# Expert stage of an attention and mixture-of-experts kernel: ten row buffers, an earlier norm and an earlier register load

## The chip, the cores and the metric

The kernel runs on one NeuronCore of a Trainium2 chip. A time is what the device takes for one execution, in microseconds (us); the time of a kernel is the median of several executions.

## The reference

4096 tokens of 128 values pass through a cross attention and then through a layer of 8 experts of which each token uses one. What matters here is the second part:

```python
idx = jnp.argmax(router_probs, axis=-1)            # one expert of 8 for each token
xn = (xt - mu) * jax.lax.rsqrt(var + LN_EPS) * ln_g + ln_b
h = jax.nn.relu(jnp.einsum('te,td,edf->tf', onehot, xn, W1) + b1[idx])     # 128 -> 512
y = jnp.einsum('te,tf,efd->td', onehot, h, W2) + b2[idx]                   # 512 -> 128
x = x + y * gates
```

## The kernel before

The first two thirds of the program compute attention and router, and scatter each token's row (its values, gate, number and the two numbers of its norm) into a table in DRAM, `rows_dram`, in which the rows of one expert stand together. A small table, `slot`, is then worked out on VectorE (DVE): for each of 39 slots (`SLOTS`) of 128 rows, which expert it belongs to and where in `rows_dram` it begins. All 8 experts' weights lie in SBUF (`WA`).

The expert stage runs over the 39 slots. Nothing but the order of code on each engine and the semaphores between them sets the order. For slot s:

- SyncE (SP) reads the slot's first row number into a register and loads 128 rows into `G[s % R]`, with R = 6 buffers. Buffer s % R is free once the result of slot s − R has been written to `out` (the waits on `g_in` and `o_out` ahead of line 287).
- DVE makes the normalised rows: `norm(s)`, line 685, from `G` into `xh`, which has two buffers.
- TensorE (PE) transposes them (line 827, "tr" below), ScalarE (ACT) copies the transpose into `xg` (line 468).
- PE multiplies with W1 in 8 matmuls (line 834, "up"); ACT applies bias and relu to half of the result (line 477), DVE to the other half in two instructions (line 697).
- PE multiplies with W2 in 8 matmuls (line 845, "down").
- DVE adds the bias (`yb`, line 704), applies the gate and the residual (`ot`, line 706; R buffers too), and GpSimd (POOL) scatters `ot` to `out` (line 388).
- The weights of the slot's expert are first copied from `WA` into one of three buffers `WR`: W1 by ACT (line 461), W2 and the biases by DVE (`stage_w2`, line 677). For the address, DVE first reads the expert's number from `slot` into a register (`value_load`, line 674).

PE's order in a step is tr(s+1), up(s), down(s−1). DVE's order in a step is:

```python
dve.wait_ge(b_up, s + 1)
norm(s + 2)
wait(dve, b_dn, s - 1)
...                                  # two relus of slot s, L697
dve.wait_ge(b_dn, t + 1)             # t = s - 1
...                                  # yb L704, ot L706 of slot s - 1
stage_w2(s + 2)                      # value_load L674, then the copy L677
```

Of the kernel before, what the change touches and what calls it, by code (L numbers as in the profile page):

```python
# [12 lines left out]
NB, S, D, H = 64, 64, 128, 16  # L13
DK = D // H
E, F = 8, 512
T = NB * S
P = 128
NP = T // P
FC = F // P
SLOTS = (T + E * (P - 1)) // P  # L20
# [14 lines left out]
def wait(eng, sem, value):  # L35

    if value > 0:
        eng.wait_ge(sem, value)
# [31 lines left out]
def build(nc, x, xT, ctxT, mask, wa, wb, wc, wpk, out):  # L70
# [4 lines left out]
    with ExitStack() as ctx:  # L75
        def sb(name, shape, dt=F32):
            return ctx.enter_context(nc.sbuf_tensor(name, shape, dt))

        def sem(name):
            return ctx.enter_context(nc.semaphore(name))  # L80
# [12 lines left out]
        ident = sb("ident", [P, P])  # L93
# [67 lines left out]
        slot = sb("slot", [1, 2, SLOTS], I32)  # L161


        R, NW, LA, NA = 6, 3, 2, 2
        xh = sb("xh", [P, 2, P])
        WA = sb("WA", [P, E, WP])
        WR = sb("WR", [P, NW, WP])
        G = sb("G", [P, R, RW])
# [5 lines left out]
        ps = ctx.enter_context(nc.psum_tensor("ps", [P, 8, 512], F32))  # L174
# [33 lines left out]
        b_tx, b_xg, b_up = sem("b_transposed"), sem("b_xT"), sem("b_up")  # L208
# [11 lines left out]
        def w1_of(s, c):  # L220
            return WR[:, s % NW, P * c:P * c + P]

        def w2_of(s, c):
            return WR[:, s % NW, F + D * c:F + D * c + D]

        def b1_of(s, c):
            return WR[:, s % NW, F + FC * D + c:F + FC * D + c + 1]

        def b2_of(s):
            return WR[:, s % NW, F + FC * D + FC:WP]  # L230

        def h_ps(s, c):
            b, k = (0, c) if c < NA else (1, c - NA)
            return ps[:, 2 * (s % 2) + b, P * k:P * k + P]
# [246 lines left out]
        def _(dve):  # L481
            v = nc.vector
# [187 lines left out]

            dve.wait_ge(s_we, 128)

            def stage_w2(s):
                ex = dve.value_load(slot[0:1, 0, s:s + 1], min_val=0, max_val=E - 1)  # L674
                wait(dve, b_dn, s - NW + 1)
                wait(dve, b_ra, NA * (s - NW + 1))
                v.tensor_copy(WR[:, s % NW:s % NW + 1, F:WP], WA[:, bass.ds(ex, 1), F:WP]).then_inc(b_w2, 1)  # L677

            stage_w2(0)
            stage_w2(1)  # L680
            def norm(t):
                q = t % R
                dve.wait_ge(g_in[q], 16 * (t // R + 1))
                wait(dve, b_tx, t - 1)
                v.tensor_scalar(xh[:, t % 2, :], G[:, q, 0:D], G[:, q, D + 3:D + 4], G[:, q, D:D + 1],  # L685
                                ALU.mult, ALU.add).then_inc(b_xh, 1)

            norm(0)
            norm(1)
            for s in range(SLOTS + 1):  # L690
                if s < SLOTS:
                    dve.wait_ge(b_up, s + 1)
                    if s + 2 < SLOTS:
                        norm(s + 2)
                    wait(dve, b_dn, s - 1)
                    for c in range(NA, FC):
                        v.tensor_scalar(hT[:, s % 2, P * c:P * c + P], h_ps(s, c), b1_of(s, c), 0.0,  # L697
                                        ALU.add, ALU.max).then_inc(b_rd, 1)
                if s >= 1:
                    t = s - 1  # L700
                    q = t % R
                    wait(dve, o_out[q], 16 * (t // R))
                    dve.wait_ge(b_dn, t + 1)
                    v.tensor_tensor(out=yb[:, t % 2, :], in0=ps[:, 6 + t % 2, 0:D], in1=b2_of(t), op=ALU.add).then_inc(b_y, 1)  # L704
                    dve.wait_ge(b_y, t + 1)
                    v.scalar_tensor_tensor(out=ot[:, q, :], in0=yb[:, t % 2, :], scalar=G[:, q, D + 2:D + 3],  # L706
                                           in1=G[:, q, 0:D], op0=ALU.mult, op1=ALU.add).then_inc(b_o, 1)
                if s + 2 < SLOTS:
                    stage_w2(s + 2)

        @block.tensor
        def _(pe):
            mm = nc.tensor.matmul

            for i in range(FIRST, LAST):
                if 0 <= i < NP:
                    q, c = i // GP % 2, P * (i % GP)
# [104 lines left out]
            for s in range(-1, SLOTS + 1):  # L822
                if s + 1 < SLOTS:
                    t = s + 1
                    pe.wait_ge(b_xh, t + 1)
                    wait(pe, b_xg, t - 1)
                    nc.tensor.transpose(ps[:, 4 + t % 2, 0:P], xh[:, t % 2, :], ident[:]).then_inc(b_tx, 1)  # L827
                if 0 <= s < SLOTS:
                    pe.wait_ge(b_w1, s + 1)
                    pe.wait_ge(b_xg, s + 1)  # L830
                    wait(pe, b_ra, NA * (s - 1))
                    wait(pe, b_rd, (FC - NA) * (s - 1))
                    for c in range(FC):
                        last = mm(h_ps(s, c), w1_of(s, c), xg[:, s % 2, :], start=True, stop=True)  # L834
                    last.then_inc(b_up, 1)
                if s >= 1:
                    t = s - 1
                    wait(pe, b_y, t - 1)
                    pe.wait_ge(b_w2, t + 1)
                    for c in range(FC):  # L840
                        if c < NA:
                            pe.wait_ge(b_ra, NA * t + c + 1)
                        else:
                            pe.wait_ge(b_rd, (FC - NA) * t + c - NA + 1)
                        last = mm(ps[:, 6 + t % 2, 0:D], hT[:, t % 2, P * c:P * c + P], w2_of(t, c),  # L845
                                  start=(c == 0), stop=(c == FC - 1))
                    last.then_inc(b_dn, 1)
# [37 lines left out]
```

## Time and profile before

| | |
|---|---|
| median of 3 runs | 316.54 us (315.61 to 317.49) |
| profiled execution, its own time | 319.22 us |
| its span, first to last instruction | 317.5 us |
| DVE busy | 220.6 us (70%) |
| PE busy | 249.2 us (79%) |
| first `xh` to last scatter's start | 213.42 to 310.38 us |

The profiled execution took 1.7 us more than its span, and 2.7 us more than the median of the others. "Busy" is the time in which an engine had an instruction at work; names such as DVEq stand for an engine's instruction queue, which handles waits and registers.

### The profile page before, as it was taken

How to read it: one execution, taken by the hardware profiler on the slowest of the kernel's cores; microseconds unless marked ns; L12 is line 12 of the kernel's file. 1: busy time of each engine (PE TensorE's matmuls, PEld its weight loads, DVE VectorE, ACT ScalarE, POOL GpSimd, SP SyncE). 2: the span in 40 equal slices, each digit the busy share in tenths (PEclk: the TensorE clock that was granted, in tenths of full speed). 3: DMA queues.
4: the chain of work that ended last, by engine and by line, in shares of the span. 5: the costliest groups of instructions: out<-in, count | busy, mean ns of one | idle time of the engine just before them, and what ended most of it. 6: DMA issues, size and time to landing. Idle time of an engine off the chain costs nothing.

```text
span 317.5 us, 8922 instructions
## 1 busy us (share of the span) xinstructions
PE 249.2 (79%) x3112; PEld 200.7 (63%) x3112; DVE 220.6 (70%) x674; ACT 177.3 (56%) x342; POOL 141.2 (44%) x158
## 2 busy tenths in 40 slices
PE   1488988998979989789898665008899999899880
PEld 0336665765857767658576664007788888788870
DVE  6517864785886979958798735814877877877870
ACT  1527784777584767576655310007667667667640
POOL 3812250541456476464672617720444434444441
PEclk9999997997997999999999955556999999999996
DMA  7999999999999940000000101111122121121110
GB/s 228 298 245 223 273 232 238 253 265 261 263 294 267 255 109 22 10 23 15 11 28 2 37 0 37 43 40 39 43 49 59 54 68 42 51 67 53 48 29 0
DMA packets 49611, 36.31 MB, mean 114 GB/s; under 512 B 3087, under 2 KB 45460, under 8 KB 49568
## 3 DMA queue, kind: packets, MB, share of 16 engines
q1 hardware_dynamic: 46864, 31.11, 43.3%
q0 software_dynamic: 2272, 4.27, 4.2%
q8 instruction: 25, 0.41, 0.5%
q10 hardware_dynamic: 432, 0.38, 0.5%
q14 instruction: 18, 0.15, 0.2%
HBM read 14.11 MB, written 22.09 MB: 114 GB/s over the span
## 4 chain that ended last, share of the span: by engine, by line
PE 38%; DVE 31%; issue 14%; ACT 5%; DVEq 3%; DMA 3%; POOL 2%; POOLq 1%; SPq 1%; ACTq 0%
PE ps L742 8%; PE ps L753 7%; DVE Pr L569 5%; PE ps L729 4%; DVE mx L549 4%; DVE xh L685 4%; DVE hT L697 4%; PE ps L803 3%; DVE ot L706 3%; PE ps L760 2%; PE ps L766 2%; PE ps L725 2%; PE ps L780 2%; DVE yb L704 2%; DVEq L674 2%
## 5 line engine op out<-in xcount | busy, mean ns | idle before, releaser
L388 POOL DMA_INDIRECT out<-ot,G x39 | 39.8, 1021 | 62.6 <-DVE ot L706 61.6
L415 ACT ACTIVATE PT<-ps 128x512 f32<-128x512 f32 x64 | 35.2, 595 | 49.7 <-PE ps L753 49.6
L549 DVE TENSOR_REDUCE mx<-ps 128x16 f32<-128x1024 f32 x32 | 39.2, 1224 | 28.6 <-PE ps L729 28.1
L742 PEld LDWEIGHTS ps<-VB,PT 128*64 128x64 f32 x1024 | 34.1, 140 | 27.1 <-issue 27.1
L742 PE MATMUL ps<-VB,PT 128*64 128x18 f32 x1024 | 36.9, 214 | 14.7 <-ACT OT L408 7.3
L834 PE MATMUL ps<-xg,WR 128*128 128x128 f32 x312 | 45.1, 289 | 0.0
L845 PE MATMUL ps<-WR,hT 128*128 128x128 f32 x312 | 41.0, 275 | 0.0
L365 POOL TENSOR_TENSOR Kb<-KT,hmask 128x512 f32<-128x512 f32 x32 | 33.2, 1042 | 17.0 <-PE ps L729 16.7
L419 ACT ACTIVATE Pr<-Pr,rowany 128x1024 f32<-128x1024 f32 x32 | 36.7, 1148 | 7.1 <-DVE Pr L569 6.0
L834 PEld LDWEIGHTS ps<-xg,WR 128*128 128x128 f32 x312 | 39.2, 197 | 1.4
L341 POOL DMA_INDIRECT rows_dram<-row,posi x32 | 32.5, 1016 | 14.3 <-DVE row L582 6.5
L569 DVE TENSOR_TENSOR Pr<-ps,mx 128x1024 f32<-128x1024 f32 x32 | 38.8, 1213 | 0.1
L845 PEld LDWEIGHTS ps<-WR,hT 128*128 128x128 f32 x312 | 37.9, 192 | 0.0
L753 PE MATMUL ps<-ident,Pr 128*128 128x128 f32 x256 | 37.5, 293 | 0.1
L468 ACT ACTIVATE xg<-ps,Wa 128x128 f32<-128x128 f32 x39 | 17.9, 458 | 27.4 <-PE ps L827 27.4
L677 DVE COPY WR<-WA 128x644 f32 x39 | 19.4, 496 | 19.8 <-issue 19.8
L461 ACT ACTIVATE WR<-WA 128x512 f32 x39 | 24.6, 630 | 14.9 <-DVE slot L668 7.7
L348 POOL TENSOR_TENSOR row<-ve,half 128x8 f32<-128x8 f32 x8 | 13.3, 1665 | 41.5 <-DVE ve L640 41.5
L753 PEld LDWEIGHTS ps<-ident,Pr 128*128 128x128 f32 x256 | 29.3, 147 | 1.5 <-ACT Pr L419 0.5
L827 PE MATMUL ps<-ident,xh 128*128 128x128 f32 x39 | 13.2, 337 | 20.2 <-DVE xh L685 17.4
L477 ACT ACTIVATE hT<-ps,WR 128x128 f32<-128x128 f32 x78 | 23.8, 355 | 2.2 <-PE ps L834 2.2
L697 DVE TENSOR_SCALAR hT<-ps,WR 128x128 f32<-128x128 f32 x78 | 23.5, 343 | 0.0
(121 smaller groups left out, 379.7 us busy)
## 6 DMA issues: line engine op xcount, KB each, us to landing
rows_dram<-empty SPq DMA_DIRECT2D x32, 528.0 KB, 10.5
WA<-in_wpk SPq DMA_DIRECT2D x8, 578.0 KB
G<-rows_dram SPq DMA_DIRECT2D x39, 66.0 KB, 1.9
X<-in_x SPq DMA_DIRECT2D x8, 256.0 KB, 7.2
C<-in_ctxT SPq DMA_DIRECT2D x8, 256.0 KB, 6.6
XT<-in_xT SPq DMA_DIRECT2D x8, 256.0 KB, 6.5
out<-ot,G POOLq DMA_INDIRECT x39, 2.3
rows_dram<-row,posi POOLq DMA_INDIRECT x32
```

The source lines that it names most:

```text
L341: g.indirect_dma_start(out=rows, out_offset=bass.IndirectOffsetOnAxis(ap=posi[:, r, k:k + 1], axis=0), in_=row[:, r, k, E:E + RW], in_offs ...
L365: g.tensor_tensor(out=Kb[:, p % 3, :, :], in0=KT[:, p // GP % 2, c:c + P][:, None, :].to_broadcast([P, 4, P]), in1=hmask[:, :, None].to_br ...
L388: g.indirect_dma_start(out=out, out_offset=bass.IndirectOffsetOnAxis(ap=G[:, q, D + 1:D + 2].bitcast(I32), axis=0), in_=ot[:, q, :], in_of ...
L415: a.activation(PT[:, p % 2, 512 * m:512 * m + 512], ps[:, 4 + m, :], ACT.Copy).then_inc(freed[4 + m], 1)
L419: a.activation(Pr[:, i % 2, :], Pr[:, i % 2, :], ACT.Exp, scale=rowany[:, 0:1]).then_inc(s_p, 1)
L549: v.tensor_reduce(out=mx[:, i % 2, :], in_=psS.rearrange("p g (i k) -> p g i k", k=S), axis=AX.X, op=ALU.max).then_inc(s_mx, 1)
L569: v.tensor_tensor(out=Pr[:, i % 2, :].rearrange("p (g i k) -> p g i k", g=4, k=S), in0=psS.rearrange("p g (i k) -> p g i k", k=S), in1=mx[ ...
L697: v.tensor_scalar(hT[:, s % 2, P * c:P * c + P], h_ps(s, c), b1_of(s, c), 0.0, ALU.add, ALU.max).then_inc(b_rd, 1)
L742: last = mm(psPV[64 * b:64 * b + 64, 18 * j:18 * j + 18], PT[:, p % 2, 128 * j + 64 * b:128 * j + 64 * b + 64], VB[:, p // GP % 3, 2 * (p ...
L753: last = nc.tensor.transpose(ps[:, 4 + m, 128 * j:128 * j + 128], Pr[:, p % 2, 128 * (4 * m + j):128 * (4 * m + j) + 128], ident[:])
L834: last = mm(h_ps(s, c), w1_of(s, c), xg[:, s % 2, :], start=True, stop=True)
L845: last = mm(ps[:, 6 + t % 2, 0:D], hT[:, t % 2, P * c:P * c + P], w2_of(t, c), start=(c == 0), stop=(c == FC - 1))
```

## The change

Three things are edited. R goes from 6 to 10, so that both `G` and `ot` have ten buffers. `xh` gets a third buffer, and DVE's norm runs three slots ahead of the relus instead of two, behind them instead of ahead of them. The register load of the expert's number is taken out of `stage_w2` and put between relu and norm. The lines below it move by two to five numbers: norm is L687 in the new kernel, relu L698, yb L709, ot L711, the W2 copy L679; the load stays L674.

```diff
-        R, NW, LA, NA = 6, 3, 2, 2
-        xh = sb("xh", [P, 2, P])
+        R, NW, LA, NA = 10, 3, 2, 2
+        xh = sb("xh", [P, 3, P])
...
-            def stage_w2(s):
-                ex = dve.value_load(slot[0:1, 0, s:s + 1], min_val=0, max_val=E - 1)
+            def expert_of(s):
+                return dve.value_load(slot[0:1, 0, s:s + 1], min_val=0, max_val=E - 1)
+
+            def stage_w2(s, ex):
...
-                wait(dve, b_tx, t - 1)
-                v.tensor_scalar(xh[:, t % 2, :], G[:, q, 0:D], G[:, q, D + 3:D + 4], G[:, q, D:D + 1],
+                wait(dve, b_tx, t - 2)
+                v.tensor_scalar(xh[:, t % 3, :], G[:, q, 0:D], G[:, q, D + 3:D + 4], G[:, q, D:D + 1],
...
+            norm(2)
             for s in range(SLOTS + 1):
                 if s < SLOTS:
                     dve.wait_ge(b_up, s + 1)
-                    if s + 2 < SLOTS:
-                        norm(s + 2)
                     wait(dve, b_dn, s - 1)
                     for c in range(NA, FC):
                         v.tensor_scalar(hT[:, s % 2, P * c:P * c + P], h_ps(s, c), b1_of(s, c), 0.0,
                                         ALU.add, ALU.max).then_inc(b_rd, 1)
+                    if s + 2 < SLOTS:
+                        ex = expert_of(s + 2)
+                    if s + 3 < SLOTS:
+                        norm(s + 3)
...
-                    stage_w2(s + 2)
+                    stage_w2(s + 2, ex)
...
-                    nc.tensor.transpose(ps[:, 4 + t % 2, 0:P], xh[:, t % 2, :], ident[:]).then_inc(b_tx, 1)
+                    nc.tensor.transpose(ps[:, 4 + t % 2, 0:P], xh[:, t % 3, :], ident[:]).then_inc(b_tx, 1)
```

On DVE, one step in the middle of the expert stage stood like this before (`b_up`, `b_down` and `b_transposed` count PE's finished ups, downs and transposes, `rows_in4` the landed rows of slot 4; "ISA" are register instructions):

```order
L685 TENSOR_SCALAR xh<-G 128x128 [waits b_transposed,rows_in4,b_up]
L697 TENSOR_SCALAR hT<-ps,WR 128x128 [waits b_down]
L697 TENSOR_SCALAR hT<-ps,WR 128x128
L704 TENSOR_TENSOR yb<-ps,WR 128x128 [waits b_down]
L706 SCALAR_TENSOR_TENSOR ot<-yb,G 128x128 [waits b_y]
L674 TENSOR_LOAD slot
L674 ISA x2
L677 ISA [waits b_relu_act,b_down]
L677 COPY WR<-WA 128x644
```

The same step on DVE in the changed kernel:

```order
L698 TENSOR_SCALAR hT<-ps,WR 128x128 [waits b_down,b_up]
L698 TENSOR_SCALAR hT<-ps,WR 128x128
L674 TENSOR_LOAD slot
L674 ISA x2
L687 TENSOR_SCALAR xh<-G 128x128 [waits b_transposed,rows_in5]
L709 TENSOR_TENSOR yb<-ps,WR 128x128 [waits b_down]
L711 SCALAR_TENSOR_TENSOR ot<-yb,G 128x128 [waits b_y]
L679 ISA [waits b_relu_act,b_down]
L679 COPY WR<-WA 128x644
```

The register load and its two register instructions have moved from between ot and the W2 copy to between relu and norm; norm has moved behind the relus and handles the rows of one slot later. Of the register work only one instruction (L679 ISA) is left between ot and the copy.

At the start of the stage DVE now reads as follows, from the norm of slot 0 to the relus of slot 1:

```order
L687 TENSOR_SCALAR xh<-G 128x128 [waits rows_in0]
L687 TENSOR_SCALAR xh<-G 128x128 [waits rows_in1]
L687 TENSOR_SCALAR xh<-G 128x128 [waits rows_in2]
L698 TENSOR_SCALAR hT<-ps,WR 128x128 [waits b_up]
L698 TENSOR_SCALAR hT<-ps,WR 128x128
L674 TENSOR_LOAD slot
L674 ISA x2
L687 TENSOR_SCALAR xh<-G 128x128 [waits b_transposed,rows_in3]
L679 ISA
L679 COPY WR<-WA 128x644
L698 TENSOR_SCALAR hT<-ps,WR 128x128 [waits b_up]
```

The third norm stood behind the wait for the first up before; it now waits for its rows alone.

## Rows read from the trace of the kernel before

**Rows 1.** The page: TensorE's granted clock in 40 slices, tenths of full speed.

```profile
PEclk9999997997997999999999955556999999999996
```

**Rows 2.** Busy time in a stretch: PE, PEld, DVE, ACT, POOL, then clock, DMA.

```profile
224.00:304.00 80.00, 75.11 (x577) 67.67 (x576) 61.50 (x203) 54.18 (x137) 34.88 (x34) 1.00 0.19 53
```

**Rows 3.** Groups of 224 to 304 us: busy, mean ns, idle before, releaser.

```profile
L677 DVE COPY WR<-WA 128x644 f32 x34 | 16.9, 497 | 17.2 <-issue 17.2
L827 PE MATMUL ps<-ident,xh 128*128 128x128 f32 x34 | 11.2, 328 | 4.9 <-DVE xh L685 2.1
```

**Rows 4.** DVE in order of time: start, us, line, [idle before <- releaser].

```profile
228.32 0.35 DVE L706 SCALAR_TENSOR_TENSOR ot<-yb,G 128x128 f32<-128x128 f32 x1
229.15 0.50 DVE L677 COPY WR<-WA 128x644 f32 x1 [0.48 <-issue]
229.56 0.34 DVE L685 TENSOR_SCALAR xh<-G 128x128 f32<-128x128 f32 x1
229.82 0.60 DVE L697 TENSOR_SCALAR hT<-ps,WR 128x128 f32<-128x128 f32 x2
230.34 0.28 DVE L704 TENSOR_TENSOR yb<-ps,WR 128x128 f32<-128x128 f32 x1
230.65 0.35 DVE L706 SCALAR_TENSOR_TENSOR ot<-yb,G 128x128 f32<-128x128 f32 x1
...
269.63 0.49 DVE L677 COPY WR<-WA 128x644 f32 x1 [0.83 <-issue]
```

**Rows 5.** L674 from 228.3 to 229.1 us: ns min/median/max, first and last start.

```profile
L674 DVEq TENSOR_LOAD <-slot x1: 305/305/305, 228.3 to 228.3; - x1
L674 DVEq FUSED_REGOPS  x1: 190/190/190, 228.7 to 228.7; - x1
```

**Rows 6.** DVE in order of time at slot 0.

```profile
217.47 0.34 DVE L685 TENSOR_SCALAR xh<-G 128x128 f32<-128x128 f32 x1 [2.28 <-PE ps L834]
217.73 0.60 DVE L697 TENSOR_SCALAR hT<-ps,WR 128x128 f32<-128x128 f32 x2
218.25 0.48 DVE L677 COPY WR<-WA 128x644 f32 x1
```

**Rows 7.** L674 from 217.4 to 218.2 us.

```profile
L674 DVEq TENSOR_LOAD <-slot x1: 304/304/304, 217.5 to 217.5; - x1
```

**Rows 8.** PE in order of time, slots 0 to 1.

```profile
215.51 1.92 PE L834 MATMUL ps<-xg,WR 128*128 128x128 f32 x8
217.87 0.47 PE L827 MATMUL ps<-ident,xh 128*128 128x128 f32 x1 [0.44 <-DVE xh L685]
...
219.53 1.06 PE L845 MATMUL ps<-WR,hT 128*128 128x128 f32 x8
220.43 0.27 PE L827 MATMUL ps<-ident,xh 128*128 128x128 f32 x1
220.54 1.06 PE L834 MATMUL ps<-xg,WR 128*128 128x128 f32 x8
221.43 0.83 PE L845 MATMUL ps<-WR,hT 128*128 128x128 f32 x6
```

**Rows 9.** The chain that ended last, 252 to 262 us: start, us, what.

```profile
254.09 0.36 DVE ot L706
...
255.24 2.85 DMA out<-ot,G
...
258.30 1.84 DMA G<-rows_dram
...
260.23 0.13 DVE xh L685
```

**Rows 10.** The end of the program in order of time.

```profile
308.85 0.35 DVE L706 SCALAR_TENSOR_TENSOR ot<-yb,G 128x128 f32<-128x128 f32 x1
309.10 0.97 POOL L388 DMA_INDIRECT out<-ot,G  x1 [0.71 <-issue]
310.38 0.97 POOL L388 DMA_INDIRECT out<-ot,G  x1 [0.30 <-issue]
```

**Rows 11.** Busy time as in Rows 2, a stretch of the attention stage.

```profile
48.00:52.50 4.50, 3.81 (x16) 2.85 (x15) 2.29 (x7) 2.17 (x4) 0.00 (x0) 0.62 1.20 256
```

More of the change, by code:

```diff
@@ L677, in stage_w2 @@
                 v.tensor_copy(WR[:, s % NW:s % NW + 1, F:WP], WA[:, bass.ds(ex, 1), F:WP]).then_inc(b_w2, 1)
-            stage_w2(0)
-            stage_w2(1)
+            stage_w2(0, expert_of(0))
+            stage_w2(1, expert_of(1))
             def norm(t):
```

## The prediction

> **What bounds the kernel now.** I read the busy times by stretch first. From 224 to 304 us the clock of TensorE is granted in full, and in 80 us PE is busy 75.1, DVE 61.5, ACT 54.2, POOL 34.9 us, with the DMA engines at 0.19 [rows 2]. PE looks like the bound, but matmuls are pipelined and their ends are modelled, so I went to the order of time for the length of one slot. From ot to ot it is 228.32 to 230.65, 2.33 us [rows 4]. In that slot DVE has one hole: 0.48 us ahead of the W2 copy, put down to "issue". The grouped view says that the hole is there in every slot: 17.2 us over 34 copies, 0.51 each [rows 3]. Elsewhere DVE starts one instruction right behind the other: ot to copy 0.83, copy to norm 0.41, norm to relu 0.26, two relus 0.52, yb to ot 0.31, which adds up to 2.33 us. So DVE, with its hole, sets the period, and PE waits for it: PE is idle 4.9 us over 34 transposes [rows 3], and the rest of its slack is hidden in the modelled ends.
>
> What the hole is: the register load begins at 228.3, together with ot, takes 0.305, and the register instructions behind it 0.190 and some gaps, so that the copy can start only 0.83 after ot did, although ot needs but 0.35 [rows 4, 5]. The load runs in the instruction queue, beside ot; what shows is the part that ot doesn't cover.
>
> What PE could do without waits is seen where it had none. From the down at 219.53 through tr at 220.43 and up at 220.54 to the next down at 221.43 no idle time stands ahead of any matmul [rows 8]. That is a full slot of 17 matmuls in 1.90 us, 0.112 each.
>
> **The change part by part.**
>
> *The register load.* Behind the relus it has work to hide under. The trace of before has this very order once, at slot 0, where no yb and ot exist: norm at 217.47, relus at 217.73, and the copy at 218.25 right behind them, with no idle time [rows 6]. The load began at 217.5, with the norm, while both relus were still to run [rows 7]. So the queue runs ahead of at least two instructions that wait for their engine. From the start of the load to the first instruction that needs its end are some 0.70 us (the 0.83 of ot to copy less about 0.13 for the one register instruction that stays at the copy). In the new order that instruction is norm, because the queue is in order: norm can start 0.70 after the load, the relus cover 0.52 of this, and a hole of at most 0.18 stays ahead of norm. The load no longer stands ahead of the copy, so ot to copy falls from 0.83 to about 0.27, what relu to copy took at slot 0 (218.25 less the second relu's start, which is 217.73 + 0.26) [rows 6].
>
> *DVE's slot after.* Without any hole: norm 0.26, relus 0.52, yb 0.31, ot 0.27, copy 0.41 = 1.77 us. With the whole hole of 0.18 it is 1.95. PE's slot is 1.90. But the hole shrinks when DVE is late: the wait for up is then already met when the copy starts, the relus and the load are passed on while the copy runs, and the load ends earlier against norm, as at slot 0. So DVE settles at PE's 1.90 and PE becomes the bound. I also looked at what PE would wait for: relu of slot s ends 0.6 to 0.7 after up(s), and down(s) begins about 1.0 after up(s) ended plus another up of 0.9, so over a microsecond is spare there; xh is made a whole slot before tr. yb waits for down(s−1), which ends 0.89 after up(s), and DVE gets there at 0.96 (0.70 + norm 0.26): no new wait. ACT is busy 54.18 of 80 us, 1.58 a slot of 2.33 [rows 2], below 1.90, and none of it moves.
>
> *Norm a slot further ahead, three buffers.* It costs nothing in the steady part: one norm per slot as before, and its new wait is for tr(s+1) (b_transposed at s+2), which stands ahead of up(s) on PE and so has passed when DVE comes out of its wait for up(s). What is queued behind norm is yb, ot and the copy; they would be held if G[s+3] were late (below). At the start it takes one wait away: tr(2) stood idle for 0.44 us for a norm that DVE began only after up(0) [rows 8]; now that norm is done before. These 0.44 us are at the low clock (8 matmuls of up(0) took 1.92, some 0.21 each [rows 8]), two matmuls' worth, which are then done in 0.11 each at the high clock. Gain about 0.2 us: the first down starts at 219.3 instead of 219.53.
>
> *Ten buffers.* The chain from ot(t) over the scatter, its landing and the load of G to norm(t+R) was 254.09 to 260.23, 6.14 us [rows 9], in a slot where it was just late: with R = 6 and norm two ahead there are 3 slots of 2.33 less 1.08 (norm stands that much ahead of ot in its step), 5.9 us. With three ahead and R = 10 there are 6 slots of 1.90 less about 0.6, 10.8 us. It is hidden with 4.6 us to spare. Were R still 6, there would be only 3.2 us for 6.14 and the gain would be lost, so this edit carries the other two. The two or three somewhat longer slots of before (this chain) go too. POOL needs 1.27 us from scatter to scatter when it has nothing to wait for, 309.10 to 310.38 [rows 10], well below 1.90. SP issues the same 39 loads; four more of them go out early, behind those for slots 0 to 5, where nothing is queued behind them but later loads.
>
> *What may not be covered.* Three slots of before were 0.35 longer because DVE's queue stopped for 0.35 at the copy, as at 269.63 with 0.83 idle instead of 0.48 [rows 4]. DVE at 1.77 catches up on a PE at 1.90 with 0.13 a slot, and the spare microsecond between relu and down should hide them. I allow 0.5 us in all for such things.
>
> **The sum.** Before, the last ot started at 308.85 [rows 10]. After: first down at 219.3; 37 slots of 1.90 less 0.11 for the missing last transpose bring the last but one down to 289.5; the last starts 0.89 later, at 290.4, ends 1.06 later, and yb and ot follow at 291.5 and 291.85. The gain is 17.0 us; from ot to the end nothing changes (1.53 us to the last scatter [rows 10], and its landing). The profiled execution's own 319.22 would become 302.2. It was 2.7 above the median, so against the runs it is 316.54 − 17.0 + 0.5 = **300.0 us**.
>
> The Trainium skill has a rule against this placement: "DMA: Bandwidth & Descriptors", section "Latency and other measured facts", gives a register load a floor of about 600 ns. The trace disagrees: 305 ns [rows 5]. By the rule load to norm would be about 1.0 instead of 0.70, DVE's slot 2.25, and by an estimate from that page the time some 312 us.
>
> **The rivals.**
>
> *DVE stays the bound by a little* (0.15). If the relus and the load are passed on only when the copy is done, the hole of 0.18 stays whole: 1.95 us a slot, 37 × 0.05 = 1.9 us more, and the three stops of 0.35 then count too, 1.0 more: 302.4, and up to 304 if gaps of 0.05 come on top. For it speaks that 1.95 and 1.90 are so close; against it, that the load began ahead of the relus at slot 0.
>
> *The change doesn't do what it says: the load waits until the second relu is at work* (0.07), as it began together with ot at 228.3 (where a wait for yb held it, though). Then 0.70 − 0.26 = 0.44 shows ahead of norm, DVE's slot is 1.77 + 0.44 = 2.21, and the gain 37 × 0.12 and the slots of before that waited for rows, some 6 us: 311. The one row at slot 0 speaks against it.
>
> *A transfer chain or POOL becomes the bound* (0.04): with scatters every 1.90 us landing would have to take over 4.6 us longer than the 2.85 of rows 9 to be felt. At half a microsecond a slot it would be 310 or so. The DMA engines at 0.19 speak against it.
>
> *Slower* (0.03): TensorE's clock. A slot of 17 matmuls at the lower clock, 1.2 GHz, is about 3.6 us (0.21 each), 1.7 more than forecast. The clock would have to be low for more than ten slots for the 17 us to be used up. For it speaks that it fell for a while in the attention stage with PE busy 3.81 of 4.50 us [rows 11]; against, that the whole expert stage after 219 us ran at full clock [rows 1], and PE only gets busier.
>
> *No change* within 0.5% (0.02): all of the gain is given back by a wait that I don't see.
>
> **How the numbers follow.** The forecast, PE as the bound, has 0.69, and spans 298.0 (no allowance, and PE's idle time at the start shrinking further) to 302. The range reaches over the first rival, to 305, which holds 0.8. What a measurement of this kernel can tell from no change is about 0.5%, 1.6 us; faster by more has 0.69 + 0.15 + 0.07 + 0.04 = 0.95, the same 0.02, slower 0.03.
>
> **What would show it.** In the new profile: ot to ot 1.90 us in most slots; no idle time ahead of the W2 copy; at most 0.2 ahead of norm; PE without idle time ahead of tr, and tr, up and down following at 0.11 and 0.89; no wait of norm for rows; tr(2) with no wait and the first down near 219.3; last ot near 292. Wrong would be a hole of 0.4 or more ahead of norm, yb waiting for down with DVE then late for the relus so that PE waits for hT, ACT's relu or xg turning up as what PE waits for, or a low clock after 219 us.

## The result, and the profile after

The changed kernel takes 301.52 us (median of 4 executions, 297.93 to 303.73) against 316.85 us of the kernel before beside it (315.61 to 317.49). The ratio is 0.948, with a 95% interval of 0.939 to 0.958. Run a second time, beside two of the experiments and the kernel before at 317.92 us, it was 300.03 us and 0.947 (0.941 to 0.952). All ratios and intervals in this document come from the executions in the faster of two states that the chip shows, and the medians from all executions, so that a ratio is not the quotient of the medians beside it.

The profiles put the gain in the expert stage. From the start of the first norm to the start of the last ot it took 213.42 to 308.85 us before, 95.4 us, and takes 215.11 to 293.36 us now, 78.2 us: 17.2 us less. The profiled execution reached the first norm 1.7 us later than the one of before, in code that is the same in both; how long that first part takes varies from one execution to the next by several us (first norm at 210.8 and at 216.9 us in two profiles of one and the same kernel below). The medians differ by 15.3 us in the first set and by 17.9 in the second, around the 17.2 of the stage. So below I compare this length of the stage, and the total only with its interval.

Busy time by stretch for the changed kernel, to be held against [rows 2] (PE, PEld, DVE, ACT, POOL, granted clock, share of DMA):

```profile
224.00:290.00 66.00, 66.00 (x594) 66.00 (x594) 62.37 (x209) 55.57 (x139) 33.48 (x36) 1.00 0.23 63
```

PE is at work in 66.00 of 66 us. Before, it was 75.1 of 80. The groups of the same stretch, against [rows 3]:

```profile
L679 DVE COPY WR<-WA 128x644 f32 x35 | 17.1, 489 | 0.0
...
L832 PE MATMUL ps<-ident,xh 128*128 128x128 f32 x34 | 9.3, 273 | 0.0
```

The copy has lost its 17.2 us of idle time, and the transpose its 4.9 us. DVE in order of time, against [rows 4]:

```profile
226.25 0.35 DVE L711 SCALAR_TENSOR_TENSOR ot<-yb,G 128x128 f32<-128x128 f32 x1
226.52 0.49 DVE L679 COPY WR<-WA 128x644 f32 x1
226.92 0.61 DVE L698 TENSOR_SCALAR hT<-ps,WR 128x128 f32<-128x128 f32 x2
227.67 0.35 DVE L687 TENSOR_SCALAR xh<-G 128x128 f32<-128x128 f32 x1
227.93 0.28 DVE L709 TENSOR_TENSOR yb<-ps,WR 128x128 f32<-128x128 f32 x1
228.25 0.35 DVE L711 SCALAR_TENSOR_TENSOR ot<-yb,G 128x128 f32<-128x128 f32 x1
...
230.81 0.60 DVE L698 TENSOR_SCALAR hT<-ps,WR 128x128 f32<-128x128 f32 x2
231.34 0.35 DVE L687 TENSOR_SCALAR xh<-G 128x128 f32<-128x128 f32 x1
231.60 0.28 DVE L709 TENSOR_TENSOR yb<-ps,WR 128x128 f32<-128x128 f32 x1
231.92 0.35 DVE L711 SCALAR_TENSOR_TENSOR ot<-yb,G 128x128 f32<-128x128 f32 x1
```

From ot to copy are 0.27 us instead of 0.83. The slot from 226.25 to 228.25 has a hole between relus and norm (relu pair at 226.92, norm at 227.67: 0.75, where 0.52 are needed), the one that ends at 231.92 has none (230.81 to 231.34: 0.53). The queue's rows of the two slots show what differs:

```profile
L674 DVEq TENSOR_LOAD <-slot x1: 428/428/428, 226.8 to 226.8; - x1
...
L674 DVEq TENSOR_LOAD <-slot x1: 310/310/310, 230.6 to 230.6; - x1
```

The register load took 428 ns in the first and 310 in the second, and in both it began while the copy was still at work, 0.1 and 0.2 us ahead of the relus. Over the stage it took 299 to 487 ns (median 311), where it had taken 299 to 420 (median 304) before; why it is longer in some slots is open. DVE thus goes in slots of 1.76 to 2.06 us, two of 2.23 and 2.24 apart, while PE goes evenly. PE in order of time, against [rows 8]:

```profile
244.58 0.27 PE L832 MATMUL ps<-ident,xh 128*128 128x128 f32 x1
244.69 1.06 PE L839 MATMUL ps<-xg,WR 128*128 128x128 f32 x8
245.58 1.06 PE L850 MATMUL ps<-WR,hT 128*128 128x128 f32 x8
246.47 0.27 PE L832 MATMUL ps<-ident,xh 128*128 128x128 f32 x1
```

244.58 to 246.47 is 1.89 us for a slot, what PE showed without waits at slot 1 of the kernel before. The mean over 35 slots, from ot(1) at 224.34 to ot(36) at 290.67, is 1.895.

### The profile page after: what moved, and what is told of

Its sections match the earlier page's. It is cut to its first block, busy times and chain, and to the rows that moved or that the text cites. A ratio compares the mean times of both kernels' runs of the same rounds, so it can differ in the third digit from the quotient of the medians.

```text
span 302.0 us, 8950 instructions
## 1 busy us (share of the span) xinstructions
PE 238.1 (79%) x3112; PEld 197.0 (65%) x3112; DVE 222.0 (74%) x674; ACT 176.9 (59%) x342; POOL 139.0 (46%) x158
## 4 chain that ended last, share of the span: by engine, by line
PE 62%; DVE 18%; issue 8%; ACT 5%; POOL 2%; DMA 1%; POOLq 1%; SPq 1%; DVEq 0%; ACTq 0%
PE ps L839 12%; PE ps L850 11%; PE ps L747 9%; PE ps L758 7%; DVE Pr L569 6%; PE ps L734 5%; DVE mx L549 4%; PE ps L808 3%; PE ps L785 3%; PE ps L765 3%; PE ps L730 2%; PE ps L771 2%; ACT QT L442 2%; DVE lsub L596 2%; POOL rows_dram L341 2%
## 5 line engine op out<-in xcount | busy, mean ns | idle before, releaser
L388 POOL DMA_INDIRECT out<-ot,G x39 | 37.8, 969 | 47.6 <-DVE ot L711 47.3
L839 PE MATMUL ps<-xg,WR 128*128 128x128 f32 x312 | 42.9, 282 | 0.0
L698 DVE TENSOR_SCALAR hT<-ps,WR 128x128 f32<-128x128 f32 x78 | 23.6, 344 | 1.6 <-PE ps L839 1.5
L734 PE MATMUL ps<-Kb,QT 32*64 32x256 f32 x512 | 23.4, 413 | 0.1
L355 POOL TENSOR_TENSOR rs<-ve,half 128x4 f32<-128x4 f32 x8 | 8.2, 1021 | 32.4 <-DVE ve L633 31.7
```

What stands on the lines that cost most here:

```text
L388: g.indirect_dma_start(out=out, out_offset=bass.IndirectOffsetOnAxis(ap=G[:, q, D + 1:D + 2].bitcast(I32), axis=0), in_=ot[:, q, :], in_of ...
L734: last = mm(psS[64 * b:64 * b + 64, j, :], QT[32 * j:32 * j + 32, q, c + 64 * b:c + 64 * b + 64], Kb[32 * j:32 * j + 32, i % 3, :, 64 * b: ...
```

## The experiments

In the table, "stage" is first norm to last ot, and "slot" the mean from ot to ot over 35 slots, both from the profile. The ratio is to the kernel before in the same set of runs. There are four sets: the changed kernel, e1 to e4, e5 to e8, and e9 to e11, each beside the kernel before.

| kernel | R | register load | norm ahead | stage | slot | time, median | ratio (95%) |
|---|---|---|---|---|---|---|---|
| before | 6 | behind ot | 2 | 95.4 | 2.36 | 316.9 | 1 |
| changed | 10 | behind relus | 3 | 78.2 | 1.895 | 301.5 | 0.948 (0.939 to 0.958) |
| e1 | 10 | behind ot | 2 | 94.7 | 2.33 | 317.6 | 0.986 (0.975 to 0.997) |
| e2 | 6 | behind relus | 2 | 96.4 | 2.40 | 317.8 | 1.001 (0.996 to 1.005) |
| e3 | 10 | behind relus | 2 | 78.6 | 1.898 | 299.7 | 0.936 (0.926 to 0.945) |
| e4 | 10 | behind ot | 3 | 93.7 | 2.34 | 316.4 | 0.995 (0.989 to 1.000) |
| e5 | 6 | behind relus | 3 | 123.0 | 3.19 | 349.4 | 1.085 (1.072 to 1.097) |
| e6 | 7 | behind relus | 3 | 87.9 | 2.19 | 314.9 | 2 executions |
| e7 | 10 | twice, behind relus | 3 | 92.3 | 2.29 | 319.3 | 0.988 (0.983 to 0.994) |
| e8 | 10 | behind relus, 52 matmuls in the gap | 3 | 78.8 | 1.895 | 306.0 | 0.944 (0.936 to 0.953) |
| e9 | the changed kernel again | | | 78.5 | 1.895 | 300.0 | 0.947 (0.941 to 0.952) |
| e10 | e3 again | | | 78.4 | 1.898 | 303.1 | 0.958 (0.952 to 0.964) |
| e11 | e3 with 104 matmuls in the gap | | | 78.9 | 1.898 | 301.8 | 0.946 (0.939 to 0.953) |

The kernel before was 316.85, 318.3, 323.6 and 317.9 us in the sets of the changed kernel, of e1 to e4, of e5 to e8 and of e9 to e11. So medians of different sets must not be compared.

**e1: ten buffers alone.** The kernel before with

```diff
-        R, NW, LA, NA = 6, 3, 2, 2
+        R, NW, LA, NA = 10, 3, 2, 2
```

> The kernel before with R = 10 and nothing else. Theory (DVE's 0.48 us hole ahead of the W2 copy sets the period, rows arrive just in time): ot to ot stays 2.33 us, only the waits of norm for rows go (some 0.5 us in all), first norm to last ot 94.9 us instead of 95.4, time 316. Rival (the buffers are what the kernel waited for): the period falls well below 2.33 and the time by 5 us or more.

The groups of 224 to 304 us:

```profile
L677 DVE COPY WR<-WA 128x644 f32 x34 | 16.9, 497 | 16.4 <-issue 16.4
...
L685 DVE TENSOR_SCALAR xh<-G 128x128 f32<-128x128 f32 x34 | 11.6, 342 | 0.0
```

The hole ahead of the copy is nearly the same, 16.4 us over 34 against 17.2, and the stage is 0.7 us shorter, at 2.33 us a slot. As the theory had it: the buffers are not what the kernel before waits for. The ratio of 0.986 rests on few executions (four, 313.6 to 319.5 us) and doesn't settle how much more than these 0.7 us they are worth.

**e2: the register load alone.** In the kernel before, R = 6:

```diff
+            def expert_of(s):
+                return dve.value_load(slot[0:1, 0, s:s + 1], min_val=0, max_val=E - 1)
...
                                         ALU.add, ALU.max).then_inc(b_rd, 1)
+                    if s + 2 < SLOTS:
+                        ex = expert_of(s + 2)
...
-                    stage_w2(s + 2)
+                    stage_w2(s + 2, ex)
```

> The kernel before with only the register load moved behind the relus; R = 6, norm two slots ahead as before. Theory: the hole ahead of the copy is gone, but now norm waits for rows, because three slots less 1.1 us must hold a chain of 5.7 to 6.1 us from ot to norm: 2.27 to 2.4 us a slot, first norm to last ot 91 to 95, time 312 to 316. Rival (the load alone was the bound): 1.90 us a slot and a time near 301.

The groups of 224 to 300 us, and then DVE in order of time:

```profile
L679 DVE COPY WR<-WA 128x644 f32 x31 | 15.2, 489 | 0.2 <-issue 0.2
...
L687 DVE TENSOR_SCALAR xh<-G 128x128 f32<-128x128 f32 x32 | 11.2, 349 | 17.7 <-issue 17.3 <-DMA G<-rows_dram 0.4
```

```profile
269.64 0.49 DVE L679 COPY WR<-WA 128x644 f32 x1
270.90 0.35 DVE L687 TENSOR_SCALAR xh<-G 128x128 f32<-128x128 f32 x1 [0.78 <-issue]
```

The idle time has moved from the copy, 0.2 us, to norm, 17.7 us. The view puts most of it down to "issue" and little to the DMA, but the instruction there is norm, which waits for landed rows, and e3, in which only R differs, has nothing of it. The chain that ended last in e2 names the transfers:

```profile
267.40 0.36 DVE ot L710
...
268.55 2.45 DMA out<-ot,G
...
271.20 1.58 DMA G<-rows_dram
...
273.26 0.35 DVE xh L687
```

From ot to norm are 5.86 us, inside the 5.7 to 6.1 expected. The next turn of that chain, from the ot at 274.37 to the norm at 281.56, took 7.19, with 3.87 for the landing in `out`. So single slots take 1.89 to 4.26 us. The slot is 2.40 us on average, at the upper end of what the chain of rows allowed by my sum, the stage 1.4 us longer than I expected at most, and the time of 317.8 us lies above the 312 to 316 expected. The lone edit gains nothing. This is the clearest point of the case: the load's hole and the row chain were two limits that lay close together, 2.33 and about 2.3 to 2.4 us.

**e3: both, without the earlier norm.** e2 with R = 10.

> Register load behind the relus and R = 10, norm still two slots ahead, in front of the relus. Theory (norm a slot further ahead matters at the start only): 1.90 us a slot with TensorE without idle time, first norm to last ot 78.5 us against 78.2 of the changed kernel, time 301 to 302. Rival (the earlier norm is needed): TensorE waits for xh in each slot, 2.0 us or more a slot, time above 304.

```profile
222.00:286.00 64.00, 64.00 (x576) 64.00 (x575) 61.65 (x203) 53.91 (x135) 32.45 (x35) 1.00 0.23 63
```

PE is at work in 64.00 of 64 us, a slot is 1.90 us, and all the slots but one of 1.97 lie within 0.01 of that, up to the last two. DVE in order of time shows why it goes more evenly than in the changed kernel:

```profile
239.99 0.34 DVE L687 TENSOR_SCALAR xh<-G 128x128 f32<-128x128 f32 x1
240.25 0.60 DVE L699 TENSOR_SCALAR hT<-ps,WR 128x128 f32<-128x128 f32 x2
240.89 0.29 DVE L708 TENSOR_TENSOR yb<-ps,WR 128x128 f32<-128x128 f32 x1
```

Here norm and both relus, 0.78 us, lie over the load's 0.70, and DVE loses 0.12 per slot ahead of yb (240.25 to 240.89 less 0.52), nothing more. From the first relu to yb are 0.63 us both where the load took 320 ns (at 219.1) and where it took 407 (at 222.9), so it isn't the load's doing; it fits a wait for PE's down, whose last matmul ended at 240.78, by ends that are modelled. So the earlier norm isn't needed for the gain. Whether it brings anything in all isn't shown: 78.2 us against 78.6 here, but 78.5 against 78.4 when both were run again (e9 and e10).

**e4: both other edits without the load.** The changed kernel with

```diff
-                    if s + 2 < SLOTS:
-                        ex = expert_of(s + 2)
...
-                    stage_w2(s + 2, ex)
+                    stage_w2(s + 2, expert_of(s + 2))
```

> The changed kernel with the register load put back between ot and the W2 copy; R = 10 and norm three ahead kept. Theory: the hole ahead of the copy is back, 2.33 us a slot, first norm to last ot about 94.7 us, time 315.5. Rival (the order of norm and relus gives part of the gain): 2.2 us a slot or less, time below 312.

```profile
239.90 0.50 DVE L679 COPY WR<-WA 128x644 f32 x1 [0.48 <-issue]
240.32 0.60 DVE L698 TENSOR_SCALAR hT<-ps,WR 128x128 f32<-128x128 f32 x2
240.84 0.46 DVE L687 TENSOR_SCALAR xh<-G 128x128 f32<-128x128 f32 x1
```

The hole of 0.48 us is back and with it the slot, 2.34 on average. The stage is 93.7 us, 1.0 less than in e1, at its start and end.

**e5 and e6: how many buffers.** The changed kernel with R = 6 and with R = 7.

> The changed kernel with R = 6. Theory: norm three ahead leaves only two slots less 0.6 us for the chain from ot to norm of 5.7 to 6.1 us, so a slot takes 3.2 to 3.4 us, first norm to last ot about 120 us and the time near 345, slower than the kernel before. Rival (the buffers matter little): 1.9 to 2.3 us a slot, time 301 to 316.

> The changed kernel with R = 7. Theory: three slots less 0.6 us for a chain of 5.7 to 6.1 us, 2.1 to 2.25 us a slot, first norm to last ot 86 to 91 us, time 309 to 314. Rival (the chain shortens when nothing else is late): 1.90 us a slot and a time near 301.

The groups of e5 (230 to 330 us) and then of e6 (230 to 300 us) that waited for rows:

```profile
L687 DVE TENSOR_SCALAR xh<-G 128x128 f32<-128x128 f32 x31 | 11.5, 371 | 44.9 <-DMA G<-rows_dram 44.9
```

```profile
L687 DVE TENSOR_SCALAR xh<-G 128x128 f32<-128x128 f32 x32 | 11.8, 370 | 12.8 <-DMA G<-rows_dram 11.8 <-issue 0.5
```

With six buffers a slot takes 3.19 us on average (single ones 1.76 to 5.80) and the kernel is 8.5% slower than before, in two executions of 351.7 and 347.0 us: a norm one slot earlier asks for its buffer one slot earlier. The chain that ended last in e5 shows one turn:

```profile
250.81 0.36 DVE ot L711
...
251.96 2.25 DMA out<-ot,G
...
254.41 1.79 DMA G<-rows_dram
...
256.22 0.03 DVE xh L687
```

From ot to norm are 5.41 us, of which 4.04 in two transfers. Two slots of 3.19 less 0.6 are 5.8. With seven buffers three slots less 0.6 hold it at 2.19: 6.0. Both lie in the 5.7 to 6.1 that the kernel before had given. There is no ratio for e6, whose two executions took 317.65 and 312.12 us; its stage is 87.9 us, inside the expected 86 to 91.

**e7: the load twice.** The changed kernel with a second, unused load:

```diff
                     if s + 2 < SLOTS:
+                        expert_of(s + 2)
                         ex = expert_of(s + 2)
```

> The changed kernel with the register load done twice behind the relus. Theory (the queue is in order, norm waits for the end of the register work, 0.70 us for one load): load to norm becomes about 1.3 us, DVE's slot 1.3 + 1.26 = 2.5 us with a hole of 0.7 to 0.8 ahead of norm, time 323 or so. Rival (the queue does register work wholly beside the engine's work): no more than 0.1 us a slot, time 301 to 305.

```profile
243.09 0.49 DVE L679 COPY WR<-WA 128x644 f32 x1
243.50 0.60 DVE L698 TENSOR_SCALAR hT<-ps,WR 128x128 f32<-128x128 f32 x2
244.52 0.47 DVE L687 TENSOR_SCALAR xh<-G 128x128 f32<-128x128 f32 x1 [0.42 <-issue]
```

The register loads of L674 in that slot, 242.3 to 244.6 us:

```profile
L674 DVEq TENSOR_LOAD <-slot x2: 310/312/313, 243.2 to 243.8; - x2
```

The rival, that register work lies wholly beside the engine's, falls: the second load costs 0.39 us a slot (2.29 less 1.895), 14.1 us over the stage. From the first load at 243.2 to norm at 244.52 are the 1.3 us that the expectation had. But the slot isn't 2.5 us, as I had expected, but mostly 2.27, and the time 319.3 us and not 323. The row of L674 says why: the first load began at 243.2, when the copy at 243.09 had just started and both relus (243.50) were still to come. When DVE is late, the load has the copy to hide under as well, 0.3 us more than I had put into this sum. For the changed kernel that gives the margin, by an estimate: the second load began 0.6 us after the first, so with one load the register work asks for 2.27 less 0.6, some 1.7 us a slot, below DVE's own 1.77 and PE's 1.90; where the load takes 0.1 us longer than usual, as in some slots of the changed kernel, it is about 1.8.

**e8 and e11: TensorE's clock at the first slots.** The changed kernel (e8), and e3 (e11), with transposes of the identity that nobody reads in the gap between the attention and the first slot. In e8:

```diff
+            pe.wait_ge(freed[4], NP)
+            for n in range(52):
+                if n == 24:
+                    pe.wait_ge(s_slot, 1)
+                nc.tensor.transpose(ps[:, 4, 0:P], ident[:], ident[:])
```

(the wait for `s_slot` ahead of the first slot is the one shown here). In e11 there are 18 more ahead of the last matmuls of the placement, and 62 instead of 28 behind the wait.

> The changed kernel with 52 transposes of the identity on TensorE, whose results nobody reads, in the gap between attention and the first slot: 24 while the slot table is made, 28 behind it. Theory (the first two slots run at the lower clock, because TensorE had been idle for 13 us): the clock is granted in full when the first rows come, up(0) and up(1) take 1.0 us instead of 1.9, first norm to last ot 76 to 77 us instead of 78.2, time about 1.5 us less, 300. Rival (the clock rises at the same moment as before, or falls again ahead of the first slot): no change, or later by the matmuls still queued.

> The same with TensorE kept busy up to the first slot by 104 transposes of the identity that nobody reads: 18 ahead of the last placement matmuls, 24 while the slot table is made, 62 behind it. Theory (the first two ups are slow because of the idle time ahead of them, and 52 matmuls that ended 3.8 us before the first rows were too few): clock granted in full at the first up, 1.0 us instead of 1.9 for each of the first two ups, first norm to last ot 76.5 us, time 1.5 to 2 us below the kernel without them. Rival (the queued transposes hold up the first real one, or the clock still falls): no gain, first norm to last ot 78 us or more.

Two stretches of e8, up to the first norm and from there to the end of the second up:

```profile
210.00:217.20 7.20, 3.29 (x29) 3.04 (x28) 1.46 (x4) 0.63 (x1) 2.33 (x3) 0.97 0.13 39
217.20:224.00 6.80, 5.26 (x24) 4.97 (x25) 3.01 (x9) 4.29 (x10) 0.00 (x0) 0.50 0.25 60
```

The clock did rise ahead of the first slot (0.97 of full on average), but PE then stood idle for 3.77 us until the first rows had come, and in the next stretch it was at the lower of its two levels, 1.2 GHz. The stage took 78.8 us, not the 76 to 77 expected. PE in order of time in e11:

```profile
203.90 2.84 PE L831 MATMUL ps<-ident 128*128 128x128 f32 x24
209.86 9.80 PE L831 MATMUL ps<-ident 128*128 128x128 f32 x62 [3.12 <-DVE slot L668]
219.50 0.38 PE L838 MATMUL ps<-ident,xh 128*128 128x128 f32 x2
220.41 1.13 PE L845 MATMUL ps<-xg,WR 128*128 128x128 f32 x8 [0.53 <-ACT xg L468]
```

With more of them the first up is quick, 1.13 us instead of 1.92, but the 24 went through at the high clock, left an idle time of 3.12 us, and 62 then took 9.80 us: the granted clock was 0.50 from 209.86 to 215 us and 1.00 from 216 on. They held up the first real transpose until 219.50, while xh had been begun at 216.60. Gain and loss cancel: stage 78.9 us, against 78.4 of e3 in the same set. Both attempts failed; a filling that ends neither too early nor too late wasn't found.

**e9 and e10: which is the better one?** The changed kernel and e3 side by side.

> The changed kernel once more, beside the next two on the same chip: first norm to last ot 78.2 us, 0.945 to 0.95 of the time of before.

> The kernel before with the register load behind the relus and R = 10 (norm two ahead), once more. Theory (the earlier norm is worth only its 0.2 to 0.4 us at the start): first norm to last ot 78.6 us, the time within 0.5% of the changed kernel's. Rival (it is really faster, since DVE goes evenly at 1.90 us instead of between 1.77 and 2.2): over 1 us less than the changed kernel.

In the profiles the stages are alike, 78.5 and 78.4 us. The medians are 300.0 and 303.1 us, though, 1% apart where I had expected at most 0.5%, with intervals that just touch, and in an earlier set it was e3 that had the lower ratio, 0.936. As the profiled stages don't differ, and the first norm came at 210.8 in one profile of e3 and at 216.9 in the other, I take the difference for the part ahead of the stage, which no run tests, and no order between the two kernels is shown.

## Why the prediction was right

*Forecast and result.* 300.0 us, in a range of 298 to 305; measured were 301.52 and in the second set 300.03. That the total came out within 1.5 us is in part luck, since the part ahead of the stage alone varies by more; the length of the stage is the better test.

*What bounds the kernel before: DVE with its hole.* Right. With the hole put back (e4) the slot is 2.34 again although both other edits stay, and with the buffers alone (e1) it stays at 2.33.

*The load hides behind the relus.* Right in the main; the hole ahead of norm in the changed kernel is 0 to 0.29 us, and 0.44 in one slot, against "at most 0.18". The sum took the load at 305 ns in every slot, and it took up to 487. The rival by which it wouldn't be hidden is out.

*DVE settles at PE's period.* Right: PE has no idle time in 66 us, at 1.895 us a slot against 1.90. The way there is not a slot of 1.90 each time, as the prediction had it for most slots, but slots of 1.76 to 2.06 that come to this on average. The rival with the whole hole of 0.18 in each slot (1.95) is out; the rows of L674 in the changed kernel and in e7 give the reason, the load passed on while the copy runs.

*Ten buffers carry the other two edits.* Right, and e2, e5 and e6 show it with a number each; the edit that they are needed for is the load, since the earlier norm brought no gain that the repeated runs show. I had not worked out the load with R = 6 and norm two ahead in the prediction; e2 shows that it would have brought nothing.

*Norm a slot further ahead costs nothing, and gains 0.2 us at the start.* The first down starts 5.58 us after the first norm (220.69 less 215.11), before 6.11 (219.53 less 213.42): 0.5 us. The idle time ahead of tr(2) is gone, as forecast: up(1) starts 1.92 us after up(0) instead of 2.62. Some 0.1 us of the half microsecond is not the edit's (up(0) starts 1.95 us after the first norm, before 2.09, behind rows that came closer together), and 0.3 us was given back, as the clock rose later: up(1) took 1.91 us instead of 1.56, with a granted clock of 0.50 from 219 to 221 us, where it had been 0.95 from 219 to 221 before. Over the whole stage nothing of it is left that stands out between e3 and the changed kernel (78.6 and 78.4 against 78.2 and 78.5).

*The three stops of 0.35 us.* They are still there, two of them: in the changed kernel one slot takes 2.23 us from ot to ot and one 2.24. PE isn't held up by them.

*The sum.* Forecast were 17.0 us less for the stage's end, measured 17.2 for its length. The allowance of 0.5 us for what isn't covered was not needed in the stage. The floor of about 600 ns for a register load, which the prediction cites from the Trainium skill, did not show: the median in the stage was 304 ns before, 311 in the changed kernel and 395 in e3, the longest 487. A small slip: the prediction's 1.27 us from scatter to scatter is 1.28 by [rows 10], which changes nothing.

*The clock.* It was granted in full (1.00) from 224 to 290 us, with PE at work throughout, as it had been from 224 to 304 before. That rival did not come about.

## What to carry to other kernels

When an engine shows a small hole put down to "issue" in each turn of a loop, look at its queue: if there is a register load, it can be moved behind instructions that are free to run and don't need its value, so that it runs while they do. Before such a hole is closed, work out the next limit at the new period, above all the chain through the buffers (their number less the lead of the one who fills them, times the new period): here closing the hole alone gained nothing, and more lead without more buffers cost 8.5%. The shortest stretch in which the next engine had no waits, here one slot at the start of the stage, gave the new period here to within half a per cent.

## What the runs showed of the hardware

GpSimd's scatter instruction took 1025 ns (median) in the kernel before, 1024 in e1 and 1022 in e4, but 967 to 972 in the changed kernel and in the nine others with the load behind the relus. In the first three DVE's copy of 644 columns starts 0.31 us ahead of the scatter (229.15 and 229.46 in the kernel before) and runs beside its beginning; in the changed kernel it is over by then (226.52 with 0.49 us, scatter at 227.40). The Trainium skill, "SBUF — State Buffer", section "Who interferes with whom", says that DVE and GpSimd share a pair of ports of which a copy like this takes hold for as long as it runs. The 55 ns agree with the sign; a wait for the whole overlap of 0.19 us is not seen, and that the copy is the cause is argued from the order in time, not shown.
